# Keys and queries ahead of the values, and both row-maxima reductions ahead of the keys' low parts, in a one-core decoder layer

## What is computed

```
def _L0_xattn_ref(x, embeds, Wq, bq, Wk, bk, Wv, bv, Wo, bo):
    H, D = (16, 64)
    q = (x @ Wq + bq).reshape(b, lq, H, D)
    k = (embeds @ Wk + bk).reshape(b, lk, H, D)
    v = (embeds @ Wv + bv).reshape(b, lk, H, D)
    scores = jnp.einsum('bqhd,bkhd->bhqk', q, k) * SCALE
    attn = jax.nn.softmax(scores, axis=-1)
    ctx = jnp.einsum('bhqk,bkhd->bqhd', attn, v).reshape(b, lq, AD)
    return ctx @ Wo + bo
...
    x = _layernorm(x + _L0_attn_ref(x, ...), axis=-1)
    x = _layernorm(x + _L0_xattn_ref(x, ctx_1024, ...), axis=-1)
    x = _layernorm(x + _L0_ffn_ref(x, L0_ffn_Wr, L0_ffn_W1, L0_ffn_W2), axis=-1)
```

## Time and profile before

| | us |
|---|---|
| median of 3 runs | 2688.73 (2688.66 to 2688.74) |
| the profiled execution | 2689.66 |
| its span, first to last instruction | 2687.8 |
| TensorE busy | 2632.7 (98%) |
| POOL busy | 2221.2 (83%) |
| VectorE busy | 2121.5 (79%) |
| ScalarE busy | 1742.3 (65%) |
| mean granted TensorE clock | 0.991 |

### The profile page before, as it was taken

One profiled execution on the slowest core, in us unless ns is written; L12 is line 12 of the kernel. 1 busy time (PEld: TensorE's weight loads), 2 busy tenths in 40 slices (PEclk: granted clock), 3 DMA queues, 4 the chain that ended last, 5 costly groups with the idle time before them and its releaser, 6 DMA issues.

```text
span 2687.8 us, 67747 instructions
## 1 busy us (share of the span) xinstructions
PE 2632.7 (98%) x26773; PEld 2265.3 (84%) x26773; DVE 2121.5 (79%) x4217; ACT 1742.3 (65%) x3511; POOL 2221.2 (83%) x1828
## 2 busy tenths in 40 slices
PE   5999999999999999999999999999999999999996
PEld 5888888888888888888888888888888888888874
DVE  5788878887787887888878788888778887777763
ACT  3766766667666676666766667666666666666742
POOL 2888988888888888888888888888888888888855
PEclk7999999999999999999999999999999999999998
DMA  4000100001000000000000010000100000000030
GB/s 103 11 19 8 24 14 14 20 11 24 11 17 17 18 16 15 18 12 21 15 13 18 10 28 10 14 19 11 24 10 17 16 14 18 9 11 10 8 106 26
DMA packets 154862, 53.25 MB, mean 20 GB/s; under 512 B 112049, under 2 KB 152236, under 8 KB 154545
## 3 DMA queue, kind: packets, MB, share of 16 engines
q1 hardware_dynamic: 149376, 45.28, 7.4%
q0 software_dynamic: 2048, 3.64, 0.4%
q10 hardware_dynamic: 3120, 0.01, 0.1%
HBM read 40.76 MB, written 8.72 MB: 18 GB/s over the span
## 4 chain that ended last, share of the span: by engine, by line
PE 95%; DVE 2%; POOL 1%; issue 1%; DMA 0%; ACT 0%; SPq 0%; POOLq 0%; DVEq 0%; ACTq 0%
PE ps L1675 26%; PE ps L1643 22%; PE ps L1639 10%; PE ps L1630 5%; PE ps L1621 4%; PE ps L1622 4%; PE ps L1623 4%; PE ps L1599 3%; PE ps L1601 3%; PE ps L1600 3%; PE ps L1691 3%; PE ps L1715 2%; PE ps L1574 1%; POOL out_dram L821 1%; PE ps L1846 1%
## 5 line engine op out<-in xcount | busy, mean ns | idle before, releaser
L740 POOL TENSOR_TENSOR key_sums<-key_sums,prob_T 65x512 f32<-65x512 f32 x1398 | 1812.2, 1296 | 158.4 <-ACT prob_T L960 0.4
L1205 DVE TENSOR_REDUCE mx<-ps 128x1 f32<-128x400 f32 (+1 forms) x2048 | 1057.7, 569 | 235.1 <-PE ps L1630 189.9
L960 ACT ACTIVATE prob_T<-ps 128x512 f32<-128x512 f32 x1536 | 833.7, 596 | 85.0 <-PE ps L1643 57.1
L1675 PE MATMUL ps<-prob_T,v_sb 128*64 128x256 f32 (+1 forms) x6656 | 740.5, 379 | 0.8 <-ACT prob_T L960 0.8
L1643 PE MATMUL ps<-q_hi,k_hi 64*128 64x256 f32 (+1 forms) x3328 | 729.7, 278 | 0.0
L1643 PE MATMUL ps<-q_lo,k_hi 64*128 64x256 f32 (+1 forms) x3328 | 728.9, 278 | 0.0
L1643 PE MATMUL ps<-q_hi,k_lo 64*128 64x256 f32 (+1 forms) x3328 | 727.5, 277 | 0.0
L1675 PEld LDWEIGHTS ps<-prob_T,v_sb 128*64 128x64 f32 (+1 forms) x6656 | 478.2, 137 | 241.5 <-ACT prob_T L960 1.7
L1643 PEld LDWEIGHTS ps<-q_hi,k_hi 64*128 64x128 f32 (+1 forms) x3328 | 578.3, 181 | 2.1 <-ACT prob_T L960 1.5
L1630 PE MATMUL ps<-k_hi,q_hi 64*128 64x400 f32 (+1 forms) x2048 | 574.1, 351 | 1.2 <-DVE q_lo L1196 1.2
L1639 PE MATMUL ps<-shift,shift_w 64*128 64x512 f32 (+1 forms) x1792 | 553.4, 381 | 3.9 <-ACT shift L931 3.9
(11 more groups left out here) (239 smaller groups left out, 3645.9 us busy)
## 6 DMA issues: line engine op xcount, KB each, us to landing
shift_f<-row_shifts SPq DMA_DIRECT2D x256, 64.0 KB
ctx_raw<-in_ctx_dram SPq DMA_DIRECT2D x120, 100.0 KB
row_shifts<-nm_T SPq DMA_DIRECT2D x512, 0.5 KB
prob_T<-in_L_ffn_W_dram SPq DMA_DIRECT2D x12, 256.0 KB, 4.9
slots_in<-no_row SPq DMA_DIRECT2D x1, 2080.0 KB, 14.3
x_in<-in_x_dram SPq DMA_DIRECT2D x8, 256.0 KB, 3.0
out_dram<-x1s SPq DMA_DIRECT2D x16, 128.0 KB, 1.9
v_sb<-slots_in SPq DMA_DIRECT2D x6, 260.0 KB, 3.1
```

Source lines behind the costliest of these rows:

```text
L740: op = nc.gpsimd.tensor_tensor(acc[0:rows, :, :], acc[0:rows, :, :], prob_T[0:rows, :, k, :], ALU.add)
L960: nc.scalar.activation(prob_T[:, h, 2 * i - 2:2 * i, :].rearrange("p k t -> p (k t)"), ps[:, bank, :], ACT.Exp).then_inc(ring_act, 1)
L1205: v.tensor_reduce(mx[:, qt, h, c:c + 1], ps[:, at.bank("mx", r, c, qt, h), 0:WID[c]], AX.X, ALU.max).then_inc(ring_dve, 1)
L1675: last = mm(ps[h * DH:h * DH + DH, bank, 0:T], v_sb[0:rows, r % NJ // 2 % 2, k, v0 + h * DH:v0 + h * DH + DH], prob_T[0:rows, h, k, :], st ...
```

## The change

In the whole-array stretch the four key chunks and the queries now stand ahead of all value fills; before, a value fill and a key chunk took turns. The same order is written in four places: the order of fills, ScalarE's read-outs, TensorE's products, and (by the list of fills) the banks. On VectorE both `row_shift` calls now stand ahead of the four low parts; before, the second one, with the transpose, stood behind the first low part. No instruction is added, removed or resized. Outside the main loop (start and end) nothing is moved.

```diff
@@ all_fills
             some = value_fills(s) if after else []
-            for i in range(4):
-                if i < len(some):
-                    put("act", "v", 4 * b + some[i][1], some[i][2])
-                if after:
-                    put("dve", "k", r + 2, i)
             if after:
+                for c in range(4):
+                    put("dve", "k", r + 2, c)
                 put("dve", "q", r + 2)
+            for _, g, n in some:
+                put("act", "v", 4 * b + g, n)
...
@@ ScalarE, batch
-                    for i in range(4):
-                        if i < len(some):
-                            values_out(at, *some[i][1:])
-                        if after:
-                            keys_high(at, s + 2, i)
                     if after:
+                        for c in range(4):
+                            keys_high(at, s + 2, c)
                         queries_high(at, s + 2)
+                    for fill in some:
+                        values_out(at, *fill[1:])
...
@@ VectorE, batch
                         maxima(at, s + 1, MAX_UNITS)
                         row_shift(at, s + 1, 0)
+                        row_shift(at, s + 1, 1)
                     for c in range(4):
                         if after:
                             keys_low(at, s + 2, c)
-                        if c == 0 and following:
-                            row_shift(at, s + 1, 1)
...
@@ TensorE, batch
-                    for i in range(4):
-                        if i < len(some):
-                            values(at, *some[i][1:])
-                        if after:
-                            keys(at, s + 2, i)
                     if after:
+                        for c in range(4):
+                            keys(at, s + 2, c)
                         queries(at, s + 2)
+                    for fill in some:
+                        values(at, *fill[1:])
```

## The result

| | before | after |
|---|---|---|
| median of 6 runs, us | 2688.11 (2686.48 to 2688.74) | 2699.16 (2697.17 to 2701.03) |
| span of the profiled execution | 2687.8 | 2697.1 |

The ratio is 1.0041, 95% interval 1.0029 to 1.0053: slower by 11 us. The page's engines, then what TensorE (PE) waited for between 66 and 2550 us: who waited for whom, us in total, times, longest. Before, that second answer had no row at all.

The account below looks back on a forecast made before the run. TensorE's own list of matmuls was taken as the bound. The terms 13.4 + 0.6 - 1.5 gave +12.5 us, a median of 2701.2 (slower by 0.46%), with a range from 2696.5 to 2711.

Parts of the forecast that it names:

- The bound and the mechanism: TensorE's matmul list bounds; its attention product would wait for VectorE's third low part, about six times, 13 us in total.
- ScalarE's and SyncE's share: High parts on ScalarE and earlier row-shift DMAs on SyncE, some 1.2 us ahead, were costed at 0 for TensorE.
- the waits inside the stretch: Places 1 to 8 of the whole-array stretch wait for the same eight score-phase fills as before: cost 0.
- The step of 0.45 from the first reduction to the first low part: On VectorE, slot 3 of batch 2: the first low part starts 0.45 us after the first reduction.
- The 0.14 from release to matmul: TensorE's first matmul behind a wait starts 0.14 us after the release.
- The big term: Slot 3 of batches 2 to 12, even: TensorE idles 2.24 us before the attention product, six times, 13.4 us.
- The bound from the start of the kernel: With scan and product as fast as at the start, POOL idle, each slot-3 wait shrinks to 0.38 us, 2.3 in all.
- The wait in slot 2 of the odd batches: Batches 1 to 13, the moments ahead of the third low part: 0.08 us each, 0.6 in all, bounds 0 to 2.1.
- What comes back in slot 4: Even batches: the score phase loses its 0.18 us hold-up as VectorE comes earlier and TensorE later; 1.5 us gained in all.
- In time: Rival: the third low part is ready for slot 3's attention product, so not slower; 2689.5 at its bound; chance 0.10.
- Faster: Rival: the earlier row shifts pay, at most 3.9 us of TensorE's waits, giving 2683.3; chance 0.02.
- The falling clock: Rival: TensorE's clock falls in the new slot-3 gaps, 2.8 us each, 16.7 more, 2717.9; chance 0.09 for some or all.

Follow-up runs that it names:

- the reduction added: The changed kernel with one more VectorE reduction over 512 columns, its result unused, ahead of the scan: 2698.42 us, ratio 1.0043.
- 64 columns added: The changed kernel with a scan over the first 64 columns ahead of the full scan: 2720.93 us, ratio 1.0129.

## Why the prediction came out right, and where its terms were off

**The bound and the mechanism** held. The attention product waits for `k_lo`, six times, 10.2 us, longest 1.7; the list foreseen was six, 13 us, longest 2.3. Some 0.2 us a wait is only the way of counting told above. It is in slot 3 of the even batches from 2 on and nowhere else; the fills make all of the loss and the row shifts nothing, shown by running each alone. ScalarE's and SyncE's share was nothing, as costed, and the waits inside the stretch too.

**The step of 0.45 from the first reduction to the first low part,** taken from the start of the kernel, is 448.35 - 447.90 = 0.45. The 0.14 from release to matmul holds as well.

**The big term was too large,** 2.24 a slot where the slots grew by 1.93: 11.6 us, not 13.4. Nearly all of that is the scan: I carried its 2.22 over the earlier trace rows, and it took 1.95. The bound from the start of the kernel, where POOL was idle, pointed the right way, and I chose the slots' value because POOL is as busy after the change. What I missed is that the scan does not slow down by a share, it waits for POOL's instruction in hand (the one that POOL has begun) to end, and so its length depends on when it starts. POOL's instruction, before:

```profile
452.46 1.28 POOL L740 TENSOR_TENSOR key_sums<-key_sums,prob_T 128x512 f32<-128x512 f32 x1
```

That one ends at 453.74, the scan at 454.81, 1.07 later. In the changed kernel:

```profile
448.97 1.29 POOL L739 TENSOR_TENSOR key_sums<-key_sums,prob_T 128x512 f32<-128x512 f32 x1
```

It ends at 450.26, the scan at 451.35: 1.09 later. With the reduction added, POOL's instruction ends at 449.31, just after the scan's start, and the scan at 450.40, again 1.09 later:

```profile
448.02 1.29 POOL L739 TENSOR_TENSOR key_sums<-key_sums,prob_T 128x512 f32<-128x512 f32 x1
```

```profile
448.47 0.67 DVE L1127 TENSOR_REDUCE pad<-kv 128x1 f32<-128x512 f32 x1
449.18 1.22 DVE L1128 TENSOR_TENSOR_SCAN work<-tables,kv 128x512 f32<-128x512 f32 x1
```

The reduction had filled a time in which the scan would have waited anyway, and the gap on TensorE stayed at 1.7. With 64 columns added it went the other way: the full scan came 0.04 behind the start of POOL's next instruction, waited for all of it and took 2.32.

```profile
449.32 1.28 POOL L739 TENSOR_TENSOR key_sums<-key_sums,prob_T 128x512 f32<-128x512 f32 x1
```

```profile
448.34 0.99 DVE L1127 TENSOR_TENSOR_SCAN work<-tables,kv 128x64 f32<-128x64 f32 x1
449.36 2.32 DVE L1128 TENSOR_TENSOR_SCAN work<-tables,kv 128x512 f32<-128x512 f32 x1
```

(449.36 + 2.32 = 451.68, and 449.32 + 1.28 = 450.60: 1.08.) All 91 scans over 512 columns beside POOL, in the eleven traces, end 1.08 to 1.09 after POOL's instruction in hand. The product takes 1.58 in both kernels: it always starts behind the scan, 1.0 us after the start of POOL's next instruction. The Trainium skill, "SBUF — State Buffer", section "Who interferes with whom", says that a VectorE instruction with two SBUF inputs contends with a GpSimd instruction that reads SBUF. These traces agree, and put a size to it: the scan takes 1.08 plus the rest of POOL's instruction, up to 2.32 us, and 1.22 alone, so it loses between nothing and 1.1 us. The low parts, which read one input from PSUM, show no such swing (0.59 to 0.64 for all 512 of the changed kernel).

**The wait in slot 2 of the odd batches,** 0.6 us in the sum, did not come: in batch 3 the last of the moments took 1.05 instead of 1.25, the third low part started at 592.27, and 0.08 was too near to nothing to be told from it. It lay within the bounds given, 0 to 2.1.

**What comes back in slot 4** was 1.2, against 1.5: batch 2's score phase is 467.17 - 459.42 = 7.75. The way there is longer than I had it: VectorE's lateness reached TensorE by ScalarE too, whose read-out `heads_raw` waited for the normalising product in eight places before and in one after:

```profile
ACT heads_raw L941 <- DVE heads_T L1245: 28.2, 8, 6.8
```

```profile
ACT heads_raw L940 <- DVE heads_T L1243: 6.8, 1, 6.8
```

**The sum** of the terms as measured is 11.6 + 0 - 1.2 = 10.4, beside 11.05 between the medians (7.8 to 14.2 by the interval of the ratio) and 12.5 forecast.

**The rivals.** "In time" needed a block of under 2.1 us from the second to the third low part; it was 4.0. "Faster" had the shifts to live on, and they buy nothing. The falling clock did not happen at gaps of 1.7 us. The gap that I had forecast was longer, about 2.0 in the way the wait list counts, and no run has one of that size in the steady part, so whether 0.09 was a fair chance for it stays open. It may be nearer than that: gaps of 3.1 us bring a fall in five of six, and 64 columns more on the scan, 0.3 us of work where POOL is idle, were enough for such a gap and cost 22 us. The rows of the first slot priced a fall rightly, 2.8 against 1.7 to 2.9 measured. The Trainium skill describes such a swing in the section named in the prediction ("TensorE: Matmul & The Clock Gate", "A second HAM failure mode: psum-queue depth-cycling"). These traces agree for gaps from 3.1 us on and not for those of 1.7.

## What to carry to other kernels

Where buffers go round in one ring over several owners, a change of order moves no work but changes who waits for whom: write down, for every fill, the one that held its buffer before and after, and look for the slots where a long instruction stands ahead of that one's release. Such a slot is cheap to mend, by a place in the order, and dear to leave, because TensorE pays for its idle time and, if it is long enough, for the clock as well. A duration read beside a busy POOL holds only for that start time; for the bounds take it alone, and alone plus one whole instruction of POOL.

## What the runs showed of the hardware

- A scan of 512 float32 columns with both inputs in SBUF ends 1.08 to 1.09 us after POOL's tensor_tensor in hand has ended, whatever its own start (1.22 alone; 1.22 to 2.32 in the slots, 91 of 91). POOL pays too: the instruction that it begins during the scan takes 2.01 instead of 1.29 and ends 1.06 after the scan (451.35), in the changed kernel

```profile
450.40 2.01 POOL L739 TENSOR_TENSOR key_sums<-key_sums,prob_T 128x512 f32<-128x512 f32 x1
```

- A dense stream of matmuls stood six idle gaps of 1.7 us in each of three kernels without a fall of the granted clock. Gaps of 3.1 and 3.3 us brought one at five of six, gaps of 3.8 at all six, in one trace each. A fall, to 1.2 GHz for 3.4 or 6.8 us, cost 1.7 to 2.9 us, about half of the time that TensorE worked at that level.
- Row shifts that were already in time came 1.2 us earlier: ScalarE's wait for them fell by 138 us in total, and the time didn't change.
